# Row gathers six tiles ahead instead of four, and ScalarE instead of VectorE copies a tile's result

## What is computed

```python
def _L1_ffn_ref(hidden_states, gate_kernel, gate_proj, up_proj, down_proj):
    x2d = hidden_states.reshape(T, D)                   # 2048 x 512
    router_logits = x2d @ gate_kernel                   # 32 experts
    routing_weights, selected_experts = jax.lax.top_k(softmax(router_logits), 8)
    routing_weights = routing_weights / jnp.sum(routing_weights, axis=-1, keepdims=True)
    ...
    sorted_inputs = jnp.take(x2d, token_rows, axis=0)   # rows in order of expert
    w0 = jax.lax.ragged_dot(sorted_inputs, gate_proj, group_sizes)
    w1 = jax.lax.ragged_dot(sorted_inputs, up_proj, group_sizes)
    inter = jax.nn.silu(w0) * w1                        # 192 wide
    expert_out = jax.lax.ragged_dot(inter, down_proj, group_sizes)
    ...
    output = jnp.einsum('BKE,BK->BE', per_token, routing_weights)
```

## Time and profile before

| | us |
|---|---|
| median of 3 runs | 1905.83 (1902.76 to 1908.11) |
| the profiled execution | 1906.77 |
| its span | 1904.9 |
| PE busy, share of the span | 1604.2 (84%) |
| DVE busy | 1195.4 (63%) |
| ACT busy | 821.2 (43%) |
| POOL busy | 1117.7 (59%) |

### The profile page before, as it was taken

How to read it: one execution, slowest core, us unless ns; L and a number is a source line. 1 busy time by engine, 2 the same in 40 slices (tenths; PEclk the granted TensorE clock), 3 DMA queues, 4 the chain that set the end, 5 groups by cost and what they waited for, 6 DMA issues and landing times. The chain is left out here.

```text
span 1904.9 us, 25083 instructions
## 1 busy us (share of the span) xinstructions
PE 1604.2 (84%) x5972; PEld 992.0 (52%) x5973; DVE 1195.4 (63%) x2157; ACT 821.2 (43%) x1211; POOL 1117.7 (59%) x576
## 2 busy tenths in 40 slices
PE   4878847999999999999999265599999999989996
PEld 2333423443444444434444154477877777777785
DVE  3656575555555565656565656876766777677674
ACT  3434435555555555555554364533323333333321
POOL 0222136887878787878797122155656566656664
PEclk9888868999999999999999565599999999999998
DMA  3222035666766676656666831278878878877775
GB/s 122 77 78 78 31 134 159 152 146 125 202 126 144 122 193 138 133 127 165 132 144 126 262 123 59 85 170 195 181 163 200 181 170 195 185 167 194 176 127 99
DMA packets 78788, 275.74 MB, mean 145 GB/s; under 512 B 11266, under 2 KB 12195, under 8 KB 66963
## 3 DMA queue, kind: packets, MB, share of 16 engines
q0 software_dynamic: 42496, 150.37, 40.4%
q1 hardware_dynamic: 36242, 124.79, 19.8%
HBM read 148.22 MB, written 126.90 MB: 144 GB/s over the span
## 5 line engine op out<-in xcount | busy, mean ns | idle before, releaser
L692 DVE TENSOR_TENSOR_SCAN B_E<-bank,B_E 128x512 f32<-128x512 f32 x256 | 306.0, 1210 | 206.4 <-ACT bank L647 199.2
L735 POOL TENSOR_TENSOR B_E<-B_E,B_Cb 128x2048 f32<-128x2048 f32 x64 | 291.9, 4561 | 110.7 <-DVE B_E L692 110.7
L1557 POOL DMA_INDIRECT out_x<-D_y,D_rows x144 | 237.7, 1650 | 172.6 <-DVE D_y L1513 118.3
L729 POOL TENSOR_TENSOR B_E<-B_dtu,B_Bb 128x2048 f32<-128x2048 f32 x64 | 292.2, 4567 | 33.7 <-DMA B_Bb<-bc_d 33.7
L608 PE MATMUL bank<-B_Wd,B_inter 128*128 128x512 f32 x512 | 230.7, 597 | 33.2 <-DVE X L686 32.3
L598 PE MATMUL bank<-hT,B_Wg 128*128 128x512 f32 x512 | 236.7, 606 | 23.3 <-DVE B_inter L681 22.2
L647 ACT ACTIVATE bank<-B_dtv,negA 128x512 f32<-128x512 f32 x256 | 171.8, 687 | 137.4 <-DVE B_E L692 136.6
L598 PE MATMUL bank<-hT,B_Wu 128*128 128x512 f32 x512 | 230.2, 592 | 0.0
L1397 ACT ACTIVATE D_sil<-bank 128x192 f32<-128x192 f32 x145 | 47.9, 330 | 400.1 <-PE bank L1340 400.1
L1334 PE MATMUL bank<-W_gu_hi,D_xT_hi 128*128 x580 | 210.6, 363 | 1.0 <-ACT D_xT_hi L1393 0.9
L1521 POOL DMA_INDIRECT D_rows<-rows_d,D_source x144 | 147.2, 1022 | 100.0 <-issue 93.0
(11 more groups left out here) (270 smaller groups left out, 2833.1 us busy)
## 6 DMA issues: line engine op xcount, KB each, us to landing
y_d<-B_E POOLq DMA_DIRECT2D x64, 1024.0 KB, 8.0
W_raw_gu<-in_wgu SPq DMA_DIRECT2D x32, 768.0 KB, 5.6
B_Bb<-bc_d SPq DMA_DIRECT2D x32, 512.0 KB, 5.3
B_Cb<-bc_d SPq DMA_DIRECT2D x32, 512.0 KB, 3.8
W_raw_d<-in_wd SPq DMA_DIRECT2D x32, 512.0 KB, 7.8
rows_d<-C_row SPq DMA_DIRECT2D x4, 1090.0 KB, 4.7
X<-in_x SPq DMA_DIRECT2D x4, 1024.0 KB, 9.0
dt_d<-A_dtv SPq DMA_DIRECT2D x4, 1024.0 KB, 3.9
```

The source lines that it names most:

```text
L692: v.tensor_tensor_scan(E[:, s % NR, c, :], dA[m % 2][:, :], E[:, s % NR, c, :], 0.0, ALU.mult, ALU.add).then_inc(s_done, 1)
L729: g.tensor_tensor(E[:, s % NR, :, :], dtu[b % 2][:, :, :], spread(Bb[jj % 2][:, s % 2, :]), ALU.mult).then_inc(dbu_done, 1)
L735: g.tensor_tensor(E[:, s % NR, :, :], E[:, s % NR, :, :], spread(Cb[jj % 2][:, s % 2, :]), ALU.mult).then_inc(prod_done, 1)
L1557: g.indirect_dma_start(a["out"], bass.IndirectOffsetOnAxis(ap=rows[i][:, ROW - 1:ROW].bitcast(U32), axis=0), ysb[:, i, :], None, compute_o ...
```

## The change

ACT instead of DVE copies `py` into `ysb`, at the end of its tile's sequence. The constant AHEAD = 6 takes the place of HALF in the gathers: six stand ahead of the loop, and in tile t POOL issues the gather of t+6, after waiting for scatter t-2 to land (before: t-4). `take` stands at the second and the sixth tile of a group, before at the fourth and the eighth. The drain's test looks only at the tile before, and its wait is for scatter t-1 alone.

```diff
+AHEAD = UNROLL - 2
...
             for i in range(UNROLL):
-                sp.wait_ge(ld_rows[i], more if i < HALF else fewer)
+                sp.wait_ge(ld_rows[i], more if i < AHEAD else fewer)
...
                             split_gate_up(act.snap(to_split[i] & (SECOND - 1), min_val=1, max_val=NE - SPLIT_AHEAD))
+                        act.wait_ge(y_ps, t + 1)
+                        act.activation(ysb[:, i, :], py[i % 2][:, :], ACT.Copy).then_inc(y_sb, 1)
...
-            for d in range(1, 3):
-                now, then = slice(d, NMETA), slice(0, NMETA - d)
...
+            now, then = slice(1, NMETA), slice(0, NMETA - 1)
...
                             fetch(v, [go], GO, ((q + 1) >> 1) * UNROLL)
-                        v.wait_ge(y_ps, t + 1)
-                        v.tensor_copy(ysb[:, ds(t & (UNROLL - 1), 1), :].rearrange("p o n -> p (o n)"), py[i % 2][:, :]).then_inc(y_sb, 1)
...
-            for i in range(HALF):
+            for i in range(AHEAD):
                 g.indirect_dma_start(rows[i], None, rows_d[:, :],
...
-                        g.wait_ge(added[i % 4], done)
+                        g.wait_ge(added[(i + 2) % 4], done + (16 if i % 4 >= 2 else 0))
                         g.sem_inc(passed)
-                        gather((i + HALF) % UNROLL)
+                        gather((i + AHEAD) % UNROLL)
                         with g.If(to_drain[i] > 0):
-                            for j in range(4):
-                                g.wait_ge(added[j], done + (16 if j < i % 4 else 0))
+                            g.wait_ge(added[(i + 3) % 4], done + (16 if i % 4 >= 1 else 0))
                             g.sem_inc(passed)
...
-                        if i % HALF == HALF - 1:
-                            take((i // HALF + 2) % 2, t + (HALF + 1))
+                        if i % HALF == 1:
+                            take(i // HALF, t + (AHEAD + 1))
                             g.wait_ge(indexed, 2 * q + (i // HALF + 2))
```

More of the change, by code:

```diff
@@ L1467, in _ @@
             step(v.tensor_copy(high, bank[6][0:1, 0:NMETA]))
-            for d in range(1, 3):
-                now, then = slice(d, NMETA), slice(0, NMETA - d)
[L1470 to L1475, removed]
+            now, then = slice(1, NMETA), slice(0, NMETA - 1)
+            step(v.tensor_tensor(part[:, now], low[:, now], high[:, then], ALU.is_le))
+            step(v.tensor_tensor(sides[:, now], low[:, then], high[:, now], ALU.is_le))
+            step(v.tensor_tensor(part[:, now], part[:, now], sides[:, now], ALU.mult))
+            step(v.tensor_tensor(sides[:, now], expert[:, now], expert[:, then], ALU.is_gt))
+            step(v.tensor_tensor(part[:, now], part[:, now], sides[:, now], ALU.mult))
+            step(v.tensor_tensor(meet[:, now], meet[:, now], part[:, now], ALU.max))
             v.tensor_copy(meta[:, DRAIN, :], meet).then_inc(drains_done, 1)
```

## The result

| kernel | median, us | runs | profiled run, us | span, us |
|---|---|---|---|---|
| before | 1905.38 | 10 | 1906.77 | 1904.9 |
| after | 1911.67 | 10 | 1910.96 | 1909.1 |

The ratio after to before is 1.0033, with a 95% interval of 1.0023 to 1.0043. The forecast was 1863 with a range of 1856 to 1882: the change makes the kernel a little slower and not 2% faster. The question is where 48 us went.

What follows compares the result with a forecast made beforehand. The prediction took PE to bound the expert stage's tile loop, with waits for gathered rows and DVE's `inner` as excess. Its sum was 1906.8 - 25 - 15 - 4.5 - 1 + 2 = 1863 us, range 1856 to 1882.

Steps and rivals of the forecast that it cites:

- Part 3, the copy's gain: DVE without the result copy starts its splits earlier: 15 us in gate/up tiles, 4.5 in down tiles, none elsewhere.
- Part 3, the copy's cost: ACT's added 599 ns copy fits ahead of silu, with 0.7 us left in gate/up tiles: costed at nothing.
- Rival (c): ACT's copy delays silu in the gate/up tiles: + 18 us, 1881; chance 0.06.
- Part 1, the lead: Gathers six ahead give some 8.5 us more lead, so PE's 25 waits for rows go: 25 of 26.0 us.
- Part 2, the new wait: POOL's wait for scatter t-2 ahead of the gather is hidden on the whole; 2 us added for thin margin.
- rival (a): Landings 0.5 us longer on average, so POOL's landing chain binds in part: about 1880; chance 0.12.
- (b): Same new wait on POOL, landings of 6.9 us on average: slower, about 1925; chance 0.06.
- upper form: POOL's turn estimated with a landing above the median and the `take` wholly on top: 4.28 us.
- (d): Waits for rows are congestion that moves along with the gathers; only the copy's gain counts: 1887; chance 0.06.
- (e): Both gains are eaten by something unseen: 1906; chance 0.02.
- Part 4: Small parts: fewer DVE ops ahead of the loop, drain test, moved `take`: about 1 us less at the end.

Runs made afterwards that it cites:

- f4: Gathers five ahead instead of four, VectorE's copy kept, against the kernel before with masked expert numbers: 1900.08 us.
- e3: ScalarE's copy and gathers five ahead, against the kernel before with masked expert numbers: 1882.10 us.
- e1_act_copy: Only the copy moved to ScalarE, gathers four ahead, against the kernel before with masked expert numbers: 1940.23 us.
- f2: ScalarE's copy and gathers five ahead, masks at the end of each PE turn, against the kernel before: 1867.55 us.
- f1: Kernel after with POOL's new wait and gather moved behind the scatter, masks behind each turn's last product: 1869.09 us.
- the base: The kernel before with expert numbers masked by register operations at their use, nothing else changed: 1909.67 us.
- c1_after_masked: The kernel after with expert numbers masked by register operations at their use: 1911.17 us.
- b3_six_ahead_dve: Gathers six ahead with the wait for scatter t-2, VectorE's copy kept, against the kernel before masked at the fetch: 1905.38 us.
- b4: The kernel after, masked at the fetch, with each weight load in the loop cut to a sixteenth: 1887.43 us.
- f3_act_copy_late_load: As e1_act_copy, but SyncE spends 16 semaphore increments, about 1 us, before the weight load: 1913.37 us.

## Why the prediction was wrong

**Part 3, the copy's gain: right for the gate/up tiles.** 15 + 4.5 = 19.5 us were forecast, 17.2 + 3.5 = 20.7 measured between before and after. The pair that differs in the copy alone, f4 and e3, gives 18.1 + 0. The 4.5 us of the down tiles are thus not borne out: in e3 the median of a down turn fell from 4.50 to 4.32, but 10 of the 30 took 4.8 us or more. Rival (c) (the prediction's text calls it the second) did not come: the gate/up turns would have shown it.

**Part 3, the copy's cost: a step was missing.** "The scatter gets its data 0.2 us earlier in a clean tile and 0.8 later in the gate/up one" was right, and I gave it no price. I asked who waits for the copy and not what else is issued next to the scatter. e1_act_copy shows the price at a lead of four: 31 us net of the gain, of which 27 go when the weight load comes 1 us later. At a lead of five the plain turns show no price at all (360.1 with either copy).

**Part 1, the lead: right in kind, too large.** The waits for rows go (f4, e3, f2, f1). Of 17.0 us in the base 9.6 came back, where I took 25 of 26: a plain turn after a stall often takes 3.95 us and not 4.25, and PE's own idle time before L1323 is less than that of its weight loads (12.4 for 17.0 us in the base). I summed the second.

**Part 2, the new wait: the step that failed.** It was taken as hidden on the whole, + 2 us. In the runs it made POOL the slowest chain of the stage, and its place ahead of the scatter alone is worth 42 us (f1_scatter_first). The formula was (L + 0.85 + 1.31) / 2, with a median L of 4.9, or with "5.7, between the median and the long ones" and 0.35 on top. Even so its upper bound, 4.28 us, lay above PE's 4.25, and I kept the 2 us. Three things were wrong in it:

- A chain that is held up by long landings wins little back at short ones, since POOL's own work fills most of the turn. I wrote "makes it good within some tiles"; but 4.25 less 3.55 leaves 0.7 a turn, and the real figure is less: a gather to the scatter takes 1.43 on average, a scatter to the gather 2.05, and a `take` 1.55 more, which is 3.87 in all and leaves 0.4. With these steps and the kernel before's own landings, one by one, the chain needs an estimated 4.34 us a tile, not 3.53 to 4.28. That is already more than PE's 4.25.
- The landings are not those of before. Their mean rose from 5.60 to 6.06 us, as rival (a) has it ("0.5 us longer on average"). With the landings of the kernel after the same working gives 4.57 us a tile. Its PE turned at 653.9 / 143 = 4.57. The trace of this run lacks semaphore updates of 94 of the 144 scatters, so 6.06 is rather too low. In c1_after_masked, where they are nearly complete, the mean is 6.28, the working gives 4.60, and PE turned at 658.2 / 143 = 4.60.
- The median of the earlier trace rows was read as the typical landing. The mean of the kernel before was 5.6, since 35 of its 144 landings take over 6.5, and the trace would have given it.

The sum closes roughly: 141 x (4.57 - 4.25) = 45 us of lag, less the lead of 8.5, leaves 37; PE idled 34.7 us before L1324. In b3_six_ahead_dve, the other kernel with the wait in front of the scatter, the stage is 653.9 us too, but that is no second proof. PE waited there for rows only four times, for 6.1 us, all behind 1740 us, and POOL's lag was 4.5 us on average: with DVE's longer split turns (286.5 us for 257.6) PE's own pace was nearly as slow as POOL's.

**The rivals.** (a) and (b) named the mechanism, with 0.12 and 0.06. Their prices, 1880 and 1925, lie on either side of the result. (b) was to decide from 6.3 us on (upper form); POOL set the pace already at 6.1 to 6.3. I weighed them by the median. The sign that I had named for part 2 being wrong, scatters many us behind ACT's copy and L1323 waiting again, is what the trace shows. (d) was wrong: the waits did not move along, as f4 shows. (e), 1906, is nearest in number, and nothing in it was unseen.

**Part 4** was to give 1 us at the end. The end took 0.4 us more; at this size nothing is shown.

**The rule of the Trainium skill.** By the figure of the Trainium skill (DMA: Bandwidth & Descriptors, § Anatomy of one DMA — SWDGE (gpsimd) path), which gives an estimate of 2.6 us for this scatter, the wait would never bind. The runs don't agree: the shortest landing with all its semaphore updates in the trace is 4.3 us, and the place of the wait alone is worth 42 us (f1).

What stays open: why the gate/up turns of f4 are longer than those of its base, why a fifth of the gate/up turns in f1 and f2 take 4.7 to 4.9 us (some 4 us in all), and why a part of the down turns are long with ACT's copy.

## What to carry to other kernels

In an in-order queue a wait belongs behind what does not need it: with the wait for t-2 in front of scatter t, landing, gather and scatter form a chain that turns in two tiles; behind it, it turns in three, and two exchanged statements were worth 42 us. Work such a chain out with each landing of the trace and the queue's own instructions, not with a median, since little of what long ones cost is won back at short ones. And when an engine's result comes 0.8 us later or earlier, look at what is issued next to it: a scatter and a load that had kept 2 us apart came to lie on each other.

## What the runs showed of the hardware

**A scatter's landing depends on what follows it.** This is read from 364 weight loads in thirteen kernels (all but b4). What sorts them is the time from the load's issue to the end of the scatter's row on POOL. Where the load is issued 0.9 us or more before that end, the scatter lands 8.1 to 11.0 us after its start (157 loads, median 9.9). In the last 0.4 us before it, the landings have a median of 7.6 (36 loads, 19 of them of f3_act_copy_late_load). From 0.2 us behind the end on, they have medians of 4.8 to 5.7 (155 loads). The next scatter lands in 6.7 to 8.6 (medians) in every case. No wait in the program joins the two.

**POOL issues a scatter more slowly behind a DVE operation with two SBUF inputs.** Where a scatter starts at least 0.1 us after the start of a split and 0.3 us before its end, its row ends 1.46 us after the split's (1.46 to 1.55 in 409 cases, over all kernels), so it takes 1.8 to 3.1 us in place of 1.58. A scatter that starts ahead of the split takes 1.58 (at most 1.64 in 315 cases), as in the earlier trace rows. Two rows of f2_five_ahead_masks_late show it:

```profile
1353.41 1.23 DVE L1515 TENSOR_TENSOR W_d_lo<-W_raw_d,W_d_hi  x1 [0.73 <-issue]
...
1353.81 2.29 POOL L1564 DMA_INDIRECT out_x<-D_y,D_rows  x1 [0.30 <-issue]
```

The Trainium skill (SBUF — State Buffer, § SBUF: two separate sides) says that the port pair which GpSimd shares with VectorE is an exclusive lock, taken also by a DVE operation with two SBUF inputs (against a GpSimd operation that reads SBUF), and that whichever starts first has it for the whole instruction. The traces agree: the scatter that comes second ends a fixed 1.46 us behind the split, as if it did next to nothing until the split was over, and the one that comes first isn't slowed.

**The clock after a long stall.** PE's granted clock fell to one half, 1.2 GHz, for 3.4 us within or right behind a wait of over 2 us for rows, six times in the kernel after and once in the kernel before. Five other waits of over 2 us in the kernel after, up to 3.1, had no such fall. One of the six:

```profile
1448.00:1451.40 3.40, 3.40 (x11) 2.84 (x11) 1.54 (x3) 1.19 (x2) 0.71 (x1) 0.50 0.97 222
```

This one follows the 2.46 us of the row of 1447.33 above. The stalled turn and the next one, less PE's wait, take 9.4 to 10.2 us together with a fall and 8.4 to 8.7 without one, after waits of the same length. So the six held PE up by about 8 us. Whether they made the stage longer is not shown, since POOL set its pace. The forecast had no term for it.
